# One-hots of the first half two pairs ahead, a second bank for turned rows, and an earlier load in a graph network on one Trainium2 core

## Reference

```python
x = layernorm(x + sage(x))   # 3 layers: mean of x[src] by dst @ Wl + bl + x @ Wr, relu between them
x = layernorm(x + gin(x))    # gelu(x[src] + edge_attr @ bond_W + bond_b) * w, sum by dst, (1+eps)x + sum, 2-layer net
x = layernorm(x + gcn(x))    # 2 layers: xw[src] * dinv[src] * ew * dinv[dst] summed by dst, self loop of weight 2,
                             # relu, layernorm, gain and shift; between them + relu(t @ Wt + bt)
x = layernorm(x + rgcn(x))   # 2 layers: h[src] @ W[type] summed by dst, + h @ loop_w + b, relu after the first
```

## Time and profile before

| what | value |
| --- | --- |
| median of 3 runs | 6355.71 us |
| profiled execution, its own time | 6339.12 us |
| its span | 6337.3 us |
| PE matmul busy | 4762.7 us (75%) |
| DVE busy | 3318.8 us (52%) |
| ACT busy | 2403.4 us (38%) |
| POOL busy | 1911.2 us (30%) |
| mean granted TensorE clock | 0.870 of full speed |

### The profile page before, as it was taken

How to read it: one execution, slowest core, us unless ns; L and a number is a source line. 1 busy time by engine, 2 the same in 40 slices (tenths; PEclk the granted TensorE clock), 3 DMA queues, 4 the chain that set the end, 5 groups by cost and what they waited for, 6 DMA issues and landing times. The chain is left out here.

```text
span 6337.3 us, 129435 instructions
## 1 busy us (share of the span) xinstructions
PE 4762.7 (75%) x25128; PEld 3037.7 (48%) x25129; DVE 3318.8 (52%) x10510; ACT 2403.4 (38%) x4967; POOL 1911.2 (30%) x1886
## 2 busy tenths in 40 slices
PE   5888678466667888867777477778588888688886
PEld 3554344233334555534444244444366665566662
DVE  4344234355544555545666466667444455576775
ACT  1333233233325777624554255555211112122333
POOL 5540661544104333015430332320133330322310
PEclk9999899777779999987888777778799999899998
DMA  3553565344323444324443244444233333233332
GB/s 103 176 174 129 166 203 185 108 140 137 127 72 121 140 140 143 124 91 133 146 145 100 80 153 159 157 155 156 80 114 115 112 109 129 89 111 115 115 102 94
DMA packets 443919, 815.61 MB, mean 129 GB/s; under 512 B 70873, under 2 KB 76819, under 8 KB 443829
## 3 DMA queue, kind: packets, MB, share of 16 engines
q1 hardware_dynamic: 389172, 697.28, 32.7%
q0 software_dynamic: 54656, 117.32, 7.3%
HBM read 480.10 MB, written 334.22 MB: 128 GB/s over the span
## 5 line engine op out<-in xcount | busy, mean ns | idle before, releaser
L1112 PE MATMUL p_agg<-onehot,msg 128*128 128x512 f16 (+1 forms) x2848 | 1226.3, 431 | 617.0 <-issue 314.0
L673 POOL DMA_INDIRECT raw<-node_s,src_i x980 | 954.6, 974 | 2030.6 <-DVE msg L1541 817.8
L1546 DVE TENSOR_SCALAR onehot<-iota,dst_f,negbase 128x512 f16<-128x512 f16 (+1 forms) x2848 | 1030.1, 415 | 982.3 <-issue 431.8
L1114 PE MATMUL p_agg<-onehot,msg 128*128 128x512 f16 (+1 forms) x2848 | 1227.7, 431 | 20.3 <-issue 19.4
L1112 PEld LDWEIGHTS p_agg<-onehot,msg 128*128 x2848 | 295.9, 104 | 1008.0 <-issue 877.4
L673 POOL DMA_INDIRECT raw<-node_x,src_i x392 | 380.1, 970 | 716.3 <-DMA feature<-more_masked 338.4
L1633 DVE BATCH_NORM_STATS2 stats<-v_ring 128x6 f32 (+1 forms) x1960 | 426.5, 280 | 201.9 <-ACT v_ring L882 97.9
L1145 PE MATMUL p_agg<-h_in,w 128*128 128x512 f32 x784 | 486.1, 706 | 59.8 <-issue 55.6
L874 ACT ACTIVATE o<-v_ring,nmr,rstd 128x128 f32 (+1 forms) x1176 | 472.2, 482 | 56.5 <-DVE nmr L1649 46.5
L1114 PEld LDWEIGHTS p_agg<-onehot,msg 128*128 x2848 | 295.5, 104 | 292.9 <-issue 129.0
L1511 DVE SCALAR_TENSOR_TENSOR hid<-type_in,p_wide 128x512 f32<-128x512 f32 (+2 forms) x456 | 257.3, 615 | 270.1 <-PE p_edge L1099 146.9
(11 more groups left out here) (260 smaller groups left out, 7831.6 us busy)
## 6 DMA issues: line engine op xcount, KB each, us to landing
node_s<-o SPq DMA_DIRECT2D x392, 256.0 KB
h_in<-feature SPq DMA_DIRECT2D x392, 256.0 KB
feature<-u SPq DMA_DIRECT2D x294, 256.0 KB
node_x<-o SPq DMA_DIRECT2D x294, 256.0 KB
res_in<-node_x SPq DMA_DIRECT2D x294, 256.0 KB
h_in<-node_s SPq DMA_DIRECT2D x196, 256.0 KB
h_t<-dinv_scratch SPq DMA_DIRECT2D x196, 256.0 KB
h_in<-in_x SPq DMA_DIRECT2D x98, 256.0 KB
```

The source lines that it names most:

```text
L673: nc.gpsimd.indirect_dma_start(out=raw[:, (e % RING) * BATCH + j, :], out_offset=None, in_=src_d, in_offset=bass.IndirectOffsetOnAxis(ap=s ...
L1112: nc.tensor.matmul(p_agg[:, a, :], tile_ap(msg, t, 0, D), oh, start=first, stop=True, skip_group_check=True)
L1114: return nc.tensor.matmul(p_agg[:, a, :], tile_ap(msg, t, D, 2 * D), oh, start=False, stop=True, skip_group_check=True)
L1546: return V.tensor_scalar(tile_ap(onehot, slot), iota[:, :], dst_f[:, bass.ds(t, 1)], negbase[:, bass.ds(it * 2 + a, 1)], ALU.subtract, ALU ...
```

## The change

A third set of three static one-hots is added. The first half of pair `it` uses places 0 to 2 when `it` is even and 10 to 12 when it is odd (`fixed_place`); the new places lie in the memory of `type_in`, which only the last two rounds use. In the first six rounds DVE no longer makes the one-hots of `(it+1, 0)` at the head of its step. Right behind those of `(it+1, 1)` it makes those of `(it+2, 0)` (`next_onehots`), and at the start of a round those of pair 1. For that it loads four list words in place of three. On the last turn of the loop `it+2` is past the end, so one set is made for nothing.

What the old order guaranteed silently is now waited for on PE: that the batches are ready (`lo_done`) before half `(it+1, 0)`, and in the third round that DVE has read the degrees of the same half of the pair before (`degrees_read`).

In the sixth round the second half's turned rows go to `p_edge`, and `turn_rows` waits only for the copy of the same half a pair earlier. In the fifth and sixth rounds SP loads `(it+2, 0)` behind the loads and residuals of its step and, in the sixth, between the two stores of turned rows, in place of `(it+1, 0)` at the head.

```diff
+THIRD = 2 * EVERY + MORE * GROUP
-        type_in = sb("type_in", [P, RING, BATCH * P], F16)
-        onehot = sb("onehot", [P, 2 * EVERY + MORE * GROUP, HALF], F16)
+        onehot = sb("onehot", [P, THIRD + RING * BATCH * P // HALF, HALF], F16)
+        type_in = onehot[:, THIRD:, :].rearrange("p s c -> p (s c)").rearrange("p (q e) -> p q e", e=BATCH * P)
+        turned_in = (p_tr[:, :], p_edge[:, :])
+        def fixed_place(it, a, j, rel):
+            if a or rel:
+                return EVERY * a + j
+            return (it % 2) * THIRD + j if isinstance(it, int) else ((it % 2) * THIRD + j).with_bounds(
+                min_val=j, max_val=THIRD + j)
...
 SP, step(it)
-                    load(it + 1, 0)
+                    if k < 4:
+                        load(it + 1, 0)
...
                             residual(it - 1, 1)
-                            store_turned(it - 3)
+                            store_turned(it - 3, 0)
+                        load(it + 2, 0)
+                        if k == 5:
+                            store_turned(it - 3, 1)
                         store_rows(it - 2)
...
 PE, items and turn_rows
                     wait_apart(pe, q.every_ready, it * 2 + (a + 1))
+                    if k == 2 and not rel:
+                        wait(pe, q.degrees_read, it * 2 + (a - 1))
                     for j in range(EVERY):
-                        item(a, (t0 + j).with_bounds(min_val=0, max_val=TILES - 1), EVERY * a + j, j == 0)
+                        item(a, (t0 + j).with_bounds(min_val=0, max_val=TILES - 1), fixed_place(it, a, j, rel), j == 0)
...
-                    wait(pe, q.turn_copied, it * 2 + a)
+                    wait(pe, q.turn_copied, it * 2 + (a - 1))
                     for b in range(4):
-                        last = nc.tensor.transpose(p_tr[:, b * P:(b + 1) * P], o[:, 4 * a + b, :], ident[:, :])
+                        last = nc.tensor.transpose(turned_in[a][:, b * P:(b + 1) * P], o[:, 4 * a + b, :], ident[:, :])
...
 PE, step(it), before half (it+1, 0)
+                            wait_apart(pe, q.lo_done, ready)
                             first_half(it + 1, 0, after)
...
 DVE
                     if k:
-                        wait(dve, q.out_done, it * 2 + (a - 1))
+                        wait(dve, q.out_done, it * 2 + (a - (1 if a or rel else 3)))
...
+                def next_onehots(it, tiles):
+                    if tiles:
+                        first_onehots(it + 1, 1, tiles[0])
+                        if not rel:
+                            first_onehots(it + 2, 0, tiles[1])
...
 DVE, gcn_step(it)
-                    if now:
-                        onehots(it + 1, now)
+                    onehots(it + 1, now)
                     scaled_sums(it, 1)
                     statistics(it - 1, 1)
                     gain_and_shift(it - 2)
-                    if now:
-                        first_onehots(it + 1, 1, after)
+                    next_onehots(it, after)
                     scale_and_move(it - 1)
```

More of the change, by code:

```diff
@@ L83, in __init__ @@
         self.lo_done = one("low", (1 + rel) * BATCHES)
-        self.every_ready = one("every", NHALF)
+        self.every_ready = one("every", NHALF + (not rel))
         self.out_done = one("out", NHALF)
@@ L99, in __init__ @@
         self.sum_made = one("sum_made", NHALF, two)
+        self.degrees_read = one("degrees_read", NHALF, part == 2 and not rel)
         self.hidden_made = one("hidden_made", 2 * NHALF, gin)
@@ L564, in next_weights, with store_turned @@
                         sp.dma_start(dst_ap, src_ap).then_inc(R[r + 1].weights_in, 16)
[L566 removed]
+                def store_turned(it, a):
                     if exists(it):
[L568 to L571 removed]
+                        wait(sp, q.turn_copied, it * 2 + (a + 1))
+                        sp.dma_start(half_block(feature[0], it, a), turned_rows[a]
+                                     ).then_inc(q.feature_stored[a].semaphore, 16)
                 def store_table(it, a):
@@ L632, in sage @@
                 load(0, 1)
+                if k >= 4:
+                    load(1, 0)
                 if r == 1:
@@ L919, in rows_turned @@
                         wait(act, q.feature_stored[a], it * 16)
-                        nc.scalar.activation(turned_rows[a], p_tr[:, :], ACT.Copy).then_inc(q.turn_copied.semaphore, 1)
+                        nc.scalar.activation(turned_rows[a], turned_in[a], ACT.Copy).then_inc(q.turn_copied.semaphore, 1)
                 def second_normalise(it):
@@ L1245, in step @@
                         else:
-                            now, after = pair_list(pe, PT, it * 2 + 1)[0]
+                            (now, after), (word, _, _) = pair_list(pe, PT, it * 2 + 1)
+                            ready = batch_in_word(pe, word)
                     elif exists(it):
@@ L1283, in step @@
                     if exists(it + 1):
-                        if rel:
-                            wait_apart(pe, q.lo_done, these[0] * 2)
+                        wait_apart(pe, q.lo_done, these[0] * 2 if rel else ready)
                         first_half(it + 1, 0, after)
@@ L1766, in sage_round @@
                     wait(dve, S[r - 1].out_done, NHALF)
+                    if rounds[r - 1].kind != RGCN:
+                        wait_apart(dve, S[r - 1].every_ready, NHALF + 1)
                 now, after = pair_list(dve, PT, 0)[0]
@@ L1769, in sage_round @@
                 first_onehots(0, 1, after[0])
+                if not rel:
+                    first_onehots(1, 0, after[3])
                 if k == 3:
```

57 lines of the change are left out of this document (30 added, 27 removed).

## The result

The changed kernel took 6463.12 us (median of 4 runs, 6446.61 to 6473.15), the kernel before 6348.49 us beside it (4 runs, 6339.82 to 6358.43). The ratio is 1.0189, 95% interval 1.0169 to 1.0209: slower by 115 us, where 18 us less were forecast. The profiled execution of the changed kernel took 6468.94 us, 129.8 us more than that of the kernel before.

A forecast was written before the change was run, and what follows sets the result against it. Waits between engines, no engine being full, were taken to bound the third, fifth and sixth rounds. Terms -34 + 36 - 10 - 15 + 5 = -18 us gave 6321.1 profiled, 6338 us as median; range 6265 to 6400 us.

The forecast's parts named there:

- +36: Sixth round: one-hots ahead of `nmr` start ACT's normalising 0.87 us later, for 41 steps, +36 us.
- The step that failed: Sixth round: the second bank removes PE's wait for the turned copy, costed at nothing as PE then waits elsewhere.
- the fourth round's -15: Fourth round: a quarter of PE's 60.9 us waiting for one-hots is gained, -15 us.
- my upper bound of +47: Fourth round: the slower bound, `nmr` later by 0.97 us in 48 steps, +47 us.
- a clock rival: Third round: a shorter wait keeps PE at 2.4 GHz, -60 us, total -78, 6278 us; chance 0.06.
- 0.25 us for a word: DVE's step: loading a fourth list word costs 0.25 us, estimated from 747 ns with three and 492 with two.
- 0.45 us for addresses: Third round, PE: computed addresses of static tiles taken at 0.45 us, between hidden and up to 1.26 a half.
- The rival on computed addresses: PE, first-half static tiles: +20 more in the third round, +36 in the first two; total +38, 6394 us; chance 0.20.
- the half-clock cover: Third round, PE: static tiles already take 0.95 us at half clock, so computed addresses hide behind the matmuls.
- the sign that I named (0.96): Third round, next profile: first-half static tiles pitch 0.96 us at full clock if addresses bind.
- -46 before the word: Fifth round: one-hots leave DVE's head, 0.97 us, into its idle time; less 0.25, times 47 steps, -34 us.
- that sign: Next profile: PE's waits for one-hots (L1109, L1112) are gone from the third to fifth rounds.

The follow-up runs named there:

- P: The kind of chip of the prediction, the result and the last ten experiments, where the kernel before took 6338 to 6348 us.
- F: The kind of chip with fast gathers, of the first eight experiments, where the kernel before took 5848 us.
- the old order with all costs: Kernel before with the third set's places, addresses, four list words and PE waits, but one-hots made at the old place: 1.0162 on P, 1.0175 on F.
- e7: Kernel before with the third set of one-hots in the fifth round alone: 0.9978 on F.
- e4: Kernel before with the third set of one-hots alone, one bank and SP's old order: 1.0090 on F.
- e3: Kernel before with only SP's new load order in the fifth and sixth rounds and the split stores: 1.0000 on F.

## Why the prediction was wrong

**By rounds, forecast against measured.** Second (and first): +5, measured +22. Third: -10, measured -5. Fourth: -15, measured +70. Fifth: -34, measured -12. Sixth: +36, measured +70. The sum was -18; the rounds and the gaps between them made +130 in the profiled executions.

**The step that failed** is the one that said of a wait taken from PE that it costs nothing: "I cost it at nothing, as PE then waits for the next one-hots or rows". PE did wait for something else, but ahead of matmuls that others wait for. That sentence is on the sixth round's second bank, which cost 8 us on P and 56 on F alone, and about 20 on P on top of the set (984.7 against 964.6). The same assumption stands behind the fourth round's -15, a quarter of 60.9 us taken as gain. Holding PE back there returned 41 of the 70 us (938.8 to 898.1), by the clock and by fewer held-back steps in shares that no run parts, and the rest is what the old order with all costs shows too (895.9, +27). The later `nmr`, my upper bound of +47 there, was worth 3 us once PE was held (898.1 to 894.7). I had a clock rival, but for a gain only, in the third round; I did not weigh it as a loss, though the earlier trace rows show what there was to lose: L1211 at 1.13 us for two matmuls, full clock.

**The costs of carrying the set** were the second failing term. I had 0.25 us for a word, 0.45 us for addresses in a third of the third round's steps, and +5 for the first two rounds. Old order with all costs measured, on P, +13, +33, +27, +21 and +4 us in the second to sixth rounds, near +98 in all. Of these the places alone made +38 to +42 and the words +19; the remainder, most in the third and fourth rounds, is with the additional waits on PE or with the combination. The rival on computed addresses added 56 us, all in the first three rounds, and nothing in the fourth and fifth, where they measured +10 to +13 and +13.

**Third round.** That the wait for degrees would take the place of that for one-hots was right, but not its size of 3.4 us: it is 57.9 us in 27 waits, 2.1 each. And PE's idle time moved here too. Ahead of the first halves it fell from 218 us to 106, and ahead of the second halves, where the kernel before has 7, it is 77, most of it with the releaser issue, which names nothing that the profile shows. Two first halves in the changed kernel's third round, late ones with long waits:

```profile
1695.57 0.56 PE L1124 MATMUL p_dense<-ecol,onehot 128*128 x4 [3.67 <-DVE deg L1646]
...
1696.91 0.29 PE L1124 MATMUL p_dense<-ecol,onehot 128*128 x4
...
1711.07 0.56 PE L1124 MATMUL p_dense<-ecol,onehot 128*128 x4 [3.41 <-DVE deg L1646]
```

The first tile behind the wait takes 0.56 us in place of 0.27, and the next follows after 1.34 in place of 0.95. I read it as registers worked out behind the wait, so that the half-clock cover that I counted on is not there for the first tile. Both terms were too small, and by luck in the same measure: from the old order to the new the early one-hots gave -36 us (768.2 to 732.3), and carrying them took +33. The following tiles keep the pitch of static places, 0.53 us at full clock where PE is busy (1852.38 to 1852.91), so the sign that I named (0.96) is not the one that shows.

**Fifth round.** The mechanism was right. From old order with all costs to the set alone it is -43 us on P and -44 on F, where I had -46 before the word. The size of the net was off by the places (+13), which I had not counted in this round. With the set alone the round is 22 us shorter, in the changed kernel 12 on P and 14 on F. The difference goes with SP's new order, which cost nothing without the set, but e7, with SP's old order, also took 665.5 us on F where e4 took 660.6; what costs it is not shown. DVE's idle time ahead of L1633's statistics became 62.0 us in 44 waits, 1.4 us each, for a forecast 1.3 and 2.28 in the earlier trace rows. But PE still waited 105.6 us for one-hots (109.2 in the earlier trace rows): that sign was wrong.

**Sixth round.** L908's wait for `nmr` is there, 54.9 us in 46 waits, 1.2 each, for a forecast 0.9. Its price is shown only in pairs 35 to 41. In the other pairs the set cost 43 us for reasons that are not shown; in the last seven PE's waits for the ring's one-hots are 8 us longer. So the near agreement of +36 with the +40 on F was luck, not proof of my reason.

**Open.** Where the 24 to 27 us of pairs 0 to 34 of the sixth round come from. How the fourth round's +27 with the old order splits (places 10 to 13, words 3, and the rest). What the second round's +22 on P holds beside the +13 of carrying the set, as that round moves by 10 us by itself. And what holds steps back on P, which has a part in most of these.

## What to carry to other kernels

In the fourth and sixth rounds of this kernel PE's idle time was not removed, only moved. Before taking a wait from PE, look where PE will stand next, and what comes behind that place: if others wait for those matmuls, the lower clock level makes them nearly twice as long (2.08 us in place of 1.12). Price what a double buffer carries with it (places from registers behind a wait, another list word, a wait for each guarantee that the order gave free) by a kernel that has all the costs and none of the benefit, and then buffer only the round that gains: here the fifth alone made 0.9978, all six 1.0238, both on F.

## What the runs showed of the hardware

Twenty matmuls that compute nothing, put in each step ahead of a wait, made a round 45 us shorter (966.9 to 921.7). The clock's mean in a round says little about its length: with fill the third round went from 0.74 to 0.86 and gained 8 us of 735.

Chips differ, and not evenly. The kernel before took 6338 to 6348 us on some and 5848 on others. Its first round took 550.0 us at 158 GB/s on P, and that of e3 463.7 us at 187 GB/s on F; their fourth rounds took 868.5 and 844.5 us. One edit (the second bank) had a ratio of 1.0002 on P and 1.0093 on F, with intervals 0.2 and 0.34% wide: a verdict of one chip on an edit of a per cent need not hold on another.
